# Split pieces of the LoRA-B operand moved ahead in the plan, one weight tile or none between the two, and the x sums of the fourth block product moved back, in an fp32-accurate two-layer kernel

## The reference

```
base  = x @ weight.T + bias                         # 2048 -> 2048, one weight for all
low   = x @ A[id7[b]].T                             # rank 16, picked for each batch element
x     = x + base + scale[id7[b]] * (low @ B[id7[b]].T)
x     = x + x @ W1[id14[b]].T                       # 2048 -> 2048, one of 16 weights for each batch element
```

## Time and profile before

| | |
|---|---|
| median of 3 runs | 2699.28 us (2698.94 to 2700.88) |
| the profiled execution's own time | 2699.46 us |
| its span, first to last instruction | 2697.7 us |
| TensorE busy | 2684.9 us, 12826 matmuls |
| VectorE, ScalarE, POOL busy | 1783.1, 1330.0, 730.6 us |
| bytes moved, mean rate | 637.91 MB, 236 GB/s |

### The profile page before, as it was taken

The page is one execution under the profiler, slowest core; times in us unless marked ns, Lnnn a source line. Parts: engine busy times, 40 slices in busy tenths (PEclk is TensorE's granted clock), DMA queues, the critical chain, the costliest instruction groups (busy, mean ns, idle before and its releaser), DMA issues.

```text
span 2697.7 us, 35566 instructions
## 1 busy us (share of the span) xinstructions
PE 2684.9 (100%) x12826; PEld 2225.8 (83%) x12826; DVE 1783.1 (66%) x1582; ACT 1330.0 (49%) x1398; POOL 730.6 (27%) x586
## 2 busy tenths in 40 slices
PE   8999999999999999999999999999999999999999
PEld 7888888888888888888888888888888888888887
DVE  7757776867555657686745565778674555667865
ACT  3423366666432326666643233566663323456665
POOL 6345621412412111150342111124034211112402
PEclk9999999999999999999999999999999999999999
DMA  8868866677645535668764554899996445489896
GB/s 296 306 234 315 296 200 211 227 274 255 223 153 172 166 110 207 212 234 271 258 208 147 173 176 145 305 311 331 370 332 207 154 158 197 139 304 312 314 321 232
DMA packets 192784, 637.91 MB, mean 236 GB/s; under 512 B 22464, under 2 KB 30816, under 8 KB 192608
## 3 DMA queue, kind: packets, MB, share of 16 engines
q1 hardware_dynamic: 185408, 609.94, 65.7%
q10 hardware_dynamic: 7200, 25.69, 2.4%
HBM read 643.93 MB, written 58.72 MB: 260 GB/s over the span
## 4 chain that ended last, share of the span: by engine, by line
PE 96%; DMA 1%; DVE 1%; issue 0%; POOL 0%; ACT 0%; ACTq 0%; SPq 0%; POOLq 0%; DVEq 0%
PE acc L966 17%; PE acc L965 17%; PE acc L967 17%; PE acc L912 14%; PE acc L913 14%; PE acc L922 14%; DMA raw<-w 1%; PE acc L875 1%; PE acc L934 1%; POOL raw L601 0%; DVE ws L836 0%; DVE ops L836 0%; PE acc L920 0%; DMA raw<-xt 0%; PE acc L891 0%
## 5 line engine op out<-in xcount | busy, mean ns | idle before, releaser
L836 DVE TENSOR_TENSOR ws<-raw,ws 128x1024 fp32r<-128x1024 f32 x1020 | 1332.2, 1330 | 438.9 <-ACT ws L710 434.1
L710 ACT CAST ws<-raw 128x1024 fp32r<-128x1024 f32 (+1 forms) x1052 | 1078.7, 1051 | 1053.1 <-PE acc L967 473.8
L965 PE MATMUL acc<-ws,ops 128*128 128x512 f32 (+1 forms) x2048 | 796.8, 389 | 0.0
L966 PE MATMUL acc<-ws,ops 128*128 128x512 f32 (+1 forms) x2048 | 796.8, 389 | 0.0
L967 PE MATMUL acc<-ws,ops 128*128 128x512 f32 (+1 forms) x2048 | 796.7, 389 | 0.0
L912 PE MATMUL acc<-ops,ws 128*128 128x512 f32 x1784 | 696.9, 391 | 1.0 <-DVE ws L836 0.6
L913 PE MATMUL acc<-ops,ws 128*128 128x512 f32 x1784 | 695.2, 390 | 0.0
L922 PE MATMUL acc<-ops,ws 128*128 128x512 f32 x1784 | 694.5, 389 | 0.0
L616 POOL TENSOR_TENSOR raw<-raw,eye_s 128x128 f32<-128x128 f32 x384 | 350.6, 942 | 1173.9 <-DMA raw<-w 1173.6
L967 PEld LDWEIGHTS acc<-ws,ops 128*128 128x128 f32 x2048 | 384.5, 188 | 79.7
L965 PEld LDWEIGHTS acc<-ws,ops 128*128 128x128 f32 x2048 | 384.5, 188 | 79.7
(11 more groups left out here) (64 smaller groups left out, 570.9 us busy)
## 6 DMA issues: line engine op xcount, KB each, us to landing
raw<-w SPq DMA_DIRECT2D x920, 512.0 KB
raw<-w_sums SPq DMA_DIRECT2D x104, 512.0 KB
raw<-xt SPq DMA_DIRECT2D x96, 512.0 KB
out<-ost SPq DMA_DIRECT2D x128, 256.0 KB, 6.8
cb<-xt SPq DMA_DIRECT2D x60, 512.0 KB, 5.8
w_sums<-raw ACTq DMA_DIRECT2D x32, 512.0 KB, 6.6
ost<-a SPq DMA_DIRECT2D x64, 128.0 KB, 3.1
x_sums<-raw ACTq DMA_DIRECT2D x16, 512.0 KB, 4.7
```

Source lines behind the costliest of these rows:

```text
L710: ins = eng.copy(hi, src)
L836: ins = eng.tensor_tensor(lo, src, hi, ALU.subtract)
L965: eng.matmul(acc, yh, wh, start=begin, stop=False)
L966: eng.matmul(acc, yh, wl, start=False, stop=False)
```

## The change

Two edits of keys, both in the loop that makes the list `splits`; nothing is added to or taken from the work. Line numbers behind the edit are two higher (L836 becomes L838).

```diff
                 key = free + 0.3 + (need - free) * (b + 0.2) / 4.6
+                if k == 3:
+                    key += 5.0
                 if k == 1:
                     key = ts[at["W", g, 0, 1]] + 4.0 + 9.0 * b
                 splits.append((key, need, "X", (g, k, b)))
...
         for i, k in enumerate(LORA_K):
             for q in range(2):
                 need = ts[at["W", g, k, 0]]
-                splits.append((need - 16.0 + q, need, "BS", (g, i, q)))
+                splits.append((need - 26.0 + 3.0 * q, need, "BS", (g, i, q)))
```

## The result

| | before | changed |
|---|---|---|
| median of 22 runs each | 2699.28 us (2697.28 to 2702.08) | 2702.81 us (2700.41 to 2706.24) |
| profiled execution, its span | 2699.46, 2697.7 us | 2703.88, 2702.1 us |

A forecast was written before the change was run, and what follows sets the result against it. The prediction took TensorE as the bound, with 1.4 us of waits behind the start. A 3.1 us wait at tile 6 less 0.77 at tile 7 gave 2.3 us lost, 2701.6 us; range 2698.6 to 2704.0.

The forecast's parts named there:

- The bound and what it allows: TensorE's waits behind the start are some 1.4 us, so no reordering can give back more than that.
- Away from tile 6: Moved LoRA-B and x pieces elsewhere count 0; groups 1 to 3 get no new wait.
- SyncE and the landings: At 77 to 95 us, counting bytes at 1.74 us a tile: tile 6 ready for POOL at 89.64, W(0,1,7).1 landing about 94.75.
- The lock: VectorE and POOL exclude each other on SBUF; two lo operations are held up, tile 6 starts at 98.85, waiting 3.1 us.
- Tile 7: TensorE asks for it 5.44 us after tile 6, at 104.3; no wait is left and the 0.77 us are gone.
- The first: Rival at tiles 6 and 7: copies fall into gaps; 2698.2 to 2699.1 us; chance 0.37 together with the third rival.
- The second: Rival at tile 7: W(0,1,7).1 waits for the first piece's lo; up to 5.4 us lost, 2704.7; over 5.4 lost 0.06.
- The third: Rival for the whole kernel: nothing measurable, everything hides, 2699.3 us; chance 0.37 together with the first rival.
- the 0.2% bound: For the whole kernel: about 0.2%, 5.4 us, is what a measurement can tell from no change; same got 0.93.

The follow-up runs named there:

- e4: The changed kernel with only the first LoRA-B pair of group 0 put back to its old place; 2698.79 us, before 2698.91.
- e12: The kernel before with only the first LoRA-B pair of group 0 put behind tile 7; 2698.07 us, ratio 0.9998 to before.
- e11: The changed kernel with the first LoRA-B pair of group 0 put behind tile 7; 2698.43 us, before 2699.04.
- e6: The changed kernel with POOL's sub of W(0,1,6) and W(0,1,7) cut to 128 of 1024 columns; 2699.07 us, before 2699.66.
- e7: The changed kernel with tile 6 between the two pieces of the first LoRA-B pair; 2701.50 us, before 2699.66.
- e2: The kernel before with only the LoRA-B pieces moved ahead, x pieces unmoved; 2703.34 us, before 2698.91.
- e3: The kernel before with only the first LoRA-B pair of group 0 moved ahead; 2702.74 us, before 2698.91.
- e10: The changed kernel with 13 fill matmuls ahead of tile 6, timed again beside the unfilled one; 2701.34 us, ratio 1.0009 to before.
- e5: The changed kernel with 13 fill matmuls ahead of tile 6, their results overwritten; 2702.07 us, before 2699.66.
- e9: The changed kernel as it is, timed again on another chip; 2702.21 us, before 2699.04.

## Why the prediction was right, and the step that it lacked

**The bound and what it allows: right.** No version's median is more than 1.5 us under before, where the waits held 1.4. The bound is one for the work behind the start; the prediction does not count the waits of 3.1 and 1.6 us in the first 10 us, which stayed as they were in every version.

**Away from tile 6: right.** e4 and e12 against e11 show that the fifteen other pairs and the x sums cost and bring nothing. Groups 1 to 3 run as before (4.42 us late at 729 us, 4.4 at the end).

**SyncE and the landings: right in size, one wait not named.** W(0,1,6).1 was issued at 82.9 us, because its buffer held the saved W(0,1,3) until that save had landed, and POOL could start at 90.25 where I had 89.64. For tile 7 I had POOL ready at 94.9 and waiting for the add until 95.35; the add was over at 95.18, and it was the transfer W(0,1,7).1 that let POOL start only at 95.69. Beside it the first piece's lo ran 0.07 us earlier than placed. Counting bytes at 1.74 us for a tile was off by 0.6 and 0.8 us, in part for a wait that I did not count.

**The lock: right, and shown.** Second piece's lo to 93.92 (predicted 94.12), add from 93.95, lo of tile 6 to 99.12 (predicted 98.82). e6 takes POOL's work away and both operations shrink. Tile 6 started at 99.17; less the 0.3 us by which this execution was late from its start, 98.9 for a predicted 98.85. The parts in between were off by some tenths in opposite directions, and the wait of 3.1 us is 2.6 to 3.9 us long in other executions with this order of the pieces, so this closeness is in part luck.

**Tile 7: no wait, as predicted, but 1.5 us late.** I wrote "TensorE asks for it 5.44 us after tile 6, at 104.3". It was 6.92 us after. This is the step that failed: it gave a TensorE that had stood still for 3 us its full clock throughout. The sum needed one more term, 1.3 to 1.6 us of clock in the profiles where it fell, and 0.14 for the first matmuls behind any such wait. With the fall in two runs of three, the median of 2702.81 is 3.5 above before and not 2.3. The runs without it, 2701.2, are where the forecast had all of them, 2.1 us lost for a predicted 2.3.

**The rivals.** The first (the copies fall in gaps) fell: the lock was met twice, and e7, which places the pieces more widely, meets it at the next tile. The second (the transfer waits for the piece) did not come: W(0,1,7).1 left at 90.61, when the first piece's lo was done, and POOL started on it 5.1 us later, and the lo of tile 7 ended at 103.18, 2.9 us ahead of its use. The third is left out by the interval, though by the 0.2% bound the change counts as the same. One number of the second is wrong: its own terms give 92.85 + 7 + 6.42 = 106.27 for a flight of 7 us, 4.3 us lost or 2703.6, and not the 2704.0 that the range takes from it. The result lies under both.

**What stays open.** Why the clock falls in one execution and not in another. It fell with waits of 3.1 us and more in three of four profiled executions, with 1.95 us in e6's and not with 1.90 us in e7's, where three of the eleven timed runs have it all the same; so the length of the wait alone does not decide. Nor does the fall keep a fixed distance to the wait: it came 0.6 us before tile 6 started in the changed kernel's profile, 0.5 us after it in e2's and e6's, and 1.2 us after it in e3's. No experiment moved a wait of one length to other places in time, so what decides is not shown. Nor is it shown why the runs with a fall are 2.1 us longer by the medians, where the clock cost tile 6 1.3 to 1.6 us; a longer wait in those runs would do it, but they have no profiles. The six runs of the kernel before with a low mean clock have no profile here, and what they waited for isn't known.

## What to carry to other kernels

When an operand with much slack is moved ahead in a list, look at what it is put in front of: its cost is nothing against its own due time and all of it against the tightest neighbour's, and on VectorE more than its own length when POOL works on SBUF then. Move such pieces behind the last tight tile, not ahead of it. Price a new wait of TensorE of some microseconds with the clock's term as well, as a chance and not as a fixed cost, and look at the mean clock of each run before trusting a median of a few.

## What the runs showed of the hardware

- With a wait of 3.1 to 3.8 us for one weight tile the granted clock went from 1.00 to 0.50, and six matmuls or more started 0.42 us or more apart in place of 0.23, in three of four profiled executions of kernels with that wait. The Trainium skill has the rate under "TensorE: Matmul & The Clock Gate", section "Wait — 56ns, not 53.3ns?", 426.7 ns from start to start for 512 columns at the low level; the trace agrees with 0.43 us.
- The fall came near the end of the wait: 0.6 us before the first matmul behind it in the changed kernel's profile (0.60 in the window from 98.5 to 99 us, with TensorE idle), 0.5 to 1.2 us after that matmul in e2's, e3's and e6's. The window from 96 to 98 us of the changed kernel, with TensorE idle for most of it, still shows 1.00. The execution in which the fall came inside the wait lost 1.3 us in tile 6, the other three 1.6.
- Thirteen matmuls without use in the wait kept the clock at 1.00 in 22 of 22 runs, though these runs are 0.4 us longer by the median than the unfilled ones without a fall. In e10's profile the added matmuls themselves held the tile up for 0.4 us.
- A VectorE lo that started while POOL's sub was at work ended 1.07 to 1.09 us after the sub did, in all 14 cases read here (the kernel before at 81.87 us; the changed kernel, e2, e3, e5, e9 and e10, two each; e7), whether it wrote 32 or 128 partitions. With the sub cut to 128 columns (e6) the two operations took 1.39 and 1.23 us.
